# Two small GpSimd steps of an attention's rescaling moved to VectorE, and another order of work at the boundary between heads

## The reference

```python
sim = jnp.einsum('bnkh,bmhk->bnhm', q, k)
attn = jax.nn.softmax(sim * scale, axis=1)
o = jnp.einsum('bnhm,bmhv->bnhv', attn, v)
x = x + ga * (o projected back to width 256)
h = _layernorm(x) * (1 + cb) + sb
x = x + gb * ffn(h)     # gate, up and down with inputs and weights rounded to blockwise FP4
```

## Time and profile before

| | us |
|---|---|
| median of the runs | 1718.21 |
| the profiled execution | 1718.21 |
| its span, first to last instruction | 1716.9 |
| PE busy | 1655.6 (96%) |
| DVE busy | 1591.8 (93%) |
| ACT busy | 1363.7 (79%) |
| POOL busy | 621.7 (36%) |

### The profile page before, as it was taken

The page is one execution under the profiler, slowest core; times in us unless marked ns, Lnnn a source line. Parts: engine busy times, 40 slices in busy tenths (PEclk is TensorE's granted clock), DMA queues, the critical chain, the costliest instruction groups (busy, mean ns, idle before and its releaser), DMA issues.

```text
span 1716.9 us, 37798 instructions
## 1 busy us (share of the span) xinstructions
PE 1655.6 (96%) x15114; PEld 813.1 (47%) x15114; DVE 1591.8 (93%) x1726; ACT 1363.7 (79%) x2488; POOL 621.7 (36%) x1339
## 2 busy tenths in 40 slices
PE   8999999999999999989999999999999989999997
PEld 6643333333333333763333332333333489999997
DVE  7889999999999999779999999999999678888886
ACT  5389999999999999559999999999999633333332
POOL 3023333333333333003633333333333365544442
PEclk9999999999999999999999999999999999999999
DMA  6102111111111112401111111111110422222200
GB/s 228 64 3 64 39 47 32 32 32 40 39 41 40 33 32 62 132 33 47 42 32 32 37 40 38 44 32 32 35 39 21 136 77 74 74 74 77 75 13 19
DMA packets 53018, 89.54 MB, mean 52 GB/s; under 512 B 3298, under 2 KB 34922, under 8 KB 52842
## 3 DMA queue, kind: packets, MB, share of 16 engines
q1 hardware_dynamic: 52426, 86.59, 15.5%
q10 hardware_dynamic: 416, 0.53, 0.1%
HBM read 57.74 MB, written 29.37 MB: 51 GB/s over the span
## 4 chain that ended last, share of the span: by engine, by line
DVE 64%; PE 30%; ACT 3%; issue 2%; POOL 1%; DMA 0%; DVEq 0%; ACTq 0%; POOLq 0%
DVE nm L1043 60%; PE slot L421 9%; PE acc L421 6%; PE acc L582 5%; PE acc L604 5%; ACT e_sb L782 2%; PE slot L638 1%; DVE ost L1056 1%; PE slot L553 1%; DVE v_sb L1004 1%; PE slot L604 1%; PE slot L437 0%; PE acc L615 0%; DVE qs L1110 0%; DVE ost L948 0%
## 5 line engine op out<-in xcount | busy, mean ns | idle before, releaser
L1043 DVE TENSOR_REDUCE nm<-slot 128x1 f32<-128x1024 f32 x1024 | 1166.4, 1215 | 7.5 <-PE slot L553 5.4
L782 ACT ACTIVATE e_sb<-slot,nm 128x1024 f32<-128x1024 f32 x1024 | 1137.4, 1113 | 22.7 <-DVE nm L1043 17.8
L582 PE MATMUL acc<-e_sb,vp 64*64 64x512 f32 x8192 | 1060.6, 594 | 7.0 <-DVE ost L1056 4.7
L553 PE MATMUL slot<-stq,stk 64*64 64x512 f16 x4096 | 411.7, 388 | 21.6 <-ACT e_sb L782 21.6
L553 PEld LDWEIGHTS slot<-stq,stk 64*64 64x64 f16 x4096 | 117.6, 103 | 626.9 <-ACT e_sb L782 589.1
L582 PEld LDWEIGHTS acc<-e_sb,vp 64*64 64x64 f32 x8192 | 283.3, 132 | 188.7 <-issue 74.8
L1259 POOL TENSOR_TENSOR dlt<-nm 128x4 f32<-128x4 f32 x128 | 25.4, 198 | 593.0 <-DVE nm L1043 593.0
L782 ACT ACTIVATION_READ_ACCUMULATOR e_sb<-slot,nm 128x1 f32 x1024 | 199.8, 195 | 0.0
L1250 POOL TENSOR_TENSOR vp<-v_sb,fac 128x512 f32<-128x512 f32 x128 | 133.4, 1042 | 10.1 <-POOL fac L1240 0.2
L1236 POOL TENSOR_TENSOR rtot<-tot,mone 128x4 f32<-128x4 f32 x128 | 131.9, 1030 | 10.0
L1230 POOL TENSOR_TENSOR wsum<-cor,ssum 128x8 f32<-128x8 f32 x128 | 25.9, 202 | 233.5 <-ACT cor L810 233.5
(11 more groups left out here) (168 smaller groups left out, 1759.6 us busy)
## 6 DMA issues: line engine op xcount, KB each, us to landing
stk<-qk_parts SPq DMA_DIRECT2D x128, 128.0 KB
o_heads<-ost SPq DMA_DIRECT2D x64, 256.0 KB, 3.4
v_sb<-o_heads SPq DMA_DIRECT2D x8, 2048.0 KB, 8.2
v_sb<-in_x SPq DMA_DIRECT2D x16, 512.0 KB, 7.7
qk_parts<-e_sb SPq DMA_DIRECT2D x32, 256.0 KB, 2.2
stq<-qk_parts SPq DMA_DIRECT2D x128, 64.0 KB
out<-e_sb SPq DMA_DIRECT2D x32, 128.0 KB, 1.7
v_sb<-in_wgu SPq DMA_DIRECT2D x1, 1408.0 KB, 14.4
```

The source lines that it names most:

```text
L553: mm = pe.matmul(slot[s][side * VD:(side + 1) * VD, c * 512:(c + 1) * 512], stk[c * 64:c * 64 + 64, h % 2, i * P + side * VD:i * P + (side ...
L582: mm = pe.matmul(acc[half * VD:(half + 1) * VD, c * 512:(c + 1) * 512], vp[rows, g % 3, gi, half, :], e_v[rows, j % ERING, n0:n0 + 512], s ...
L782: act.activation(e_v[:, j % ERING, half * 1024:(half + 1) * 1024], slot[u % 3][:, :], ACT.Exp, bias=nm[:, g % 4, i, half:half + 1], accum_ ...
L1043: dve.tensor_reduce(nm[:, g % 4, i, half:half + 1], slot[u % 3][:, :], AX.X, ALU.max, negate=True).then_inc(maxed.sem)
```

## The change

Four edits, all in the attention loop.

1. The cut-off at zero moves from POOL to DVE: at j mod 4 = 0, behind the first maximum. ACT now waits for diff_cut, which DVE signals.
2. The reciprocal of the total moves from POOL (a power of -1) to DVE (a reciprocal): at j mod 4 = 1, behind the first maximum. POOL splits its chain there: wsum and tot at j mod 4 = 0, then fac and vp at j mod 4 = 1 after a wait for rtot_made. The constant mone goes.
3. DVE's copy of acc at the end of a head moves from behind the second maximum to between the two.
4. PE no longer has the special case at the start of a head: each attend call follows its score step there too.

```diff
@@ PE
-                    begins = jv > 0 and jv % NT == 0
                     for half in range(2):
                         if j < JT:
                             scores(b, j, half)
-                        if jv >= 0 and not begins:
-                            attend(b, 2 * jv + half)
-                    if begins:
-                        attend(b, 2 * jv)
-                        attend(b, 2 * jv + 1)
+                        if j >= LAG:
+                            attend(b, 2 * (j - LAG) + half)
@@ ACT
-                        act.wait_ge(*diff_made.past(b * JG + g))
+                        act.wait_ge(*diff_cut.past(b * JG + g))
                         act.activation(cor[:, g % 4], dlt[:, g % 4], ACT.Exp).then_inc(cor_made.sem)
@@ DVE
                 for half in range(2):
+                    if half == 1 and jv >= 0 and jv % NT == NT - 1:
+                        h = jv // NT
+                        dve.wait_ge(*attended.past(b * JT + jv))
+                        if b * H + h >= 2:
+                            dve.wait_ge(*o_out[h % 2].past((b * H + h - 2) // 2))
+                        dve.tensor_copy(ost[:, h % 2, 0:512], acc[:, 0:512]).then_inc(took_low.sem)
                     if j < JT:
                         maximum(b, j, half)
-                if jv >= 0 and jv % NT == NT - 1:
...
+                    if half == 0 and j % GROUP == 0 and GROUP <= j <= JT:
+                        g = j // GROUP - 1
+                        dve.wait_ge(*diff_made.past(b * JG + g))
+                        dve.tensor_scalar(dlt[:, g % 4], dlt[:, g % 4], 0.0, None, ALU.min).then_inc(diff_cut.sem)
+                    if half == 0 and j % GROUP == 1 and GROUP <= j < JT + GROUP:
+                        g = j // GROUP - 1
+                        dve.wait_ge(*tot_made.past(b * JG + g))
+                        dve.reciprocal(rtot[:, g % 4, :], tot[:, g % 4, :]).then_inc(rtot_made.sem)
@@ POOL
-                    sem, n = pool_own.next()
-                    pool.tensor_tensor(tot[:, s, :], wsum[:, s, :, 0], wsum[:, s, :, 1], ALU.add).then_inc(sem)
-                    pool.wait_ge(sem, n)
-                    sem, n = pool_own.next()
-                    pool.tensor_tensor(rtot[:, s, :], tot[:, s, :], mone[:, :], ALU.pow).then_inc(sem)
-                    pool.wait_ge(sem, n)
+                    pool.tensor_tensor(tot[:, s, :], wsum[:, s, :, 0], wsum[:, s, :, 1], ALU.add).then_inc(tot_made.sem)
+                if j % GROUP == 1 and GROUP <= j < JT + GROUP:
                     h, i0 = divmod(GROUP * g, NT)
+                    pool.wait_ge(*rtot_made.past(b * JG + g))
...
-                    pool.tensor_tensor(dlt[:, s, :, 1], nm[:, s, :, 0], nm[:, s, :, 1], ALU.subtract).then_inc(sem)
-                    pool.wait_ge(sem, n)
-                    pool.tensor_scalar(dlt[:, s], dlt[:, s], 0.0, None, ALU.min).then_inc(diff_made.sem)
+                    pool.tensor_tensor(dlt[:, s, :, 1], nm[:, s, :, 0], nm[:, s, :, 1], ALU.subtract).then_inc(diff_made.sem)
```

More of the change, by code:

```diff
@@ L139, in adaln_block @@
         rtot = sb("rtot", [P, 4, GROUP])
-        mone = sb("mone", [P, GROUP])
         fac = sb("fac", [P, 4, GROUP, 2])
@@ L249, in adaln_block @@
         made_ident, made_half, rstd_made, wv_low = tally("made_ident"), tally("made_half"), tally("rstd_made"), tally("wv_low")
-        diff_made, vp_made = tally("diff_made"), tally("vp_made")
+        diff_made, tot_made, vp_made = tally("diff_made"), tally("tot_made"), tally("vp_made")
         wsq_made, root_made = tally("wsq_made"), tally("root_made")
@@ L265, in adaln_block @@
         rows_read, rows_made, gu_quant, dn_quant = tally("rows_read"), tally("rows_made"), tally("gu_quant"), tally("dn_quant")
-        maxed, took_low = tally("maxed"), tally("took_low")
+        maxed, diff_cut, rtot_made, took_low = tally("maxed"), tally("diff_cut"), tally("rtot_made"), tally("took_low")
         wgu_low, wdb_low, x2_made, moments = tally("wgu_low"), tally("wdb_low"), tally("x2_made"), tally("moments")
@@ L670, in tensor_program @@
                         project(1)
-                    jv = j - LAG
-                    begins = jv > 0 and jv % NT == 0
                     for half in range(2):
@@ L1317, in gpsimd_program @@
             pool.memset(quarter4[:, :, :], -0.25)
-            pool.memset(mone[:, :], -1.0)
             pool.memset(epsilon, EPS)
```

## The result

The changed kernel takes 1745.53 us (median of four runs, 1742.92 to 1745.73) against 1718.16 (four runs of the kernel before); the ratio on record is 1.0152, 95% interval 1.0135 to 1.0170, and that of the two medians 1.0159. It is 27.4 us slower. The profiled execution took 1745.73 us, its span is 1744.4, 27.5 more than before. The forecast was 1748 us.

What follows compares the result with a forecast made beforehand. DVE, running its maxima back to back every 1.131 us, was taken as the bound. Terms 21.7 + 0.5 + 7.2 + 0.5 = 29.9 us on top of 1718.21 gave 1748 us, range 1738 to 1757.

Steps and rivals of the forecast that it cites:

- Small instructions: Cut-off and reciprocal on DVE in the attention loop: 124 groups at 0.175 us each, 21.7 us more (17 to 43).
- Rival A: Small instructions on DVE don't overlap with the maxima: 124 x 0.35 = 43.4 us, kernel 1770 us; chance 0.09.
- Waits of the small instructions: In DVE's loop: neither cut-off nor reciprocal waits; the reciprocal has 0.35 us of margin behind POOL's total.
- Rival B: In the loop the reciprocal waits for POOL's total: 19 to 37 us more, kernel 1767 to 1785 us; chance 0.07.
- Folds: Second batch: POOL's folds may hold the reciprocal four times, about 0.3 us each; 0.5 us put down (0 to 1.5).
- Boundary: Between heads: the copy waits 0.44 us, the old 0.20 stall goes; +0.24 us, 30 times, 7.2 us (0 to 13).
- End of the batch: First batch's end: statistics start 2.1 us later, normalisation about 0.5 us later; +0.5 us (0 to 2).
- Rival C: The boundary between heads is cheap: 1741 us, inside the forecast's own range; chance 0.80 together with the forecast.
- D: Rival: not slower; small instructions slip into DVE's waiting time and the 0.2 us stall goes: 1712 us; chance 0.04.

Runs made afterwards that it cites:

- cut_only: The kernel before with only the cut-off at zero moved to DVE, reciprocal on POOL and boundary as before: 1726.63 us, ratio 1.0048.
- recip_only: The kernel before with only the reciprocal moved to DVE, cut-off on POOL and boundary as before: 1727.72 us, ratio 1.0054.
- late2: The changed kernel with two more totals on POOL ahead of the real one, which comes 0.56 us later: 1774.17 us, ratio 1.0321.
- copy_only: The kernel before with only DVE's copy of acc moved between the two maxima: 1728.22 us, ratio 1.0050.
- bound_only: The kernel before with both the moved copy and PE's new attend order, no small instruction moved: 1728.81 us, ratio 1.0050.
- order_only: The kernel before with only PE's new order, each attend behind its score step at a head's start too: 1725.75 us, ratio 1.0036.

## Why the prediction was right

The direction and the mechanism held, and so did the time (1748 against 1745.5), which is partly luck: 3.1 us that the sum did not have stood in for terms that it had too high. Without them the time would be about 1742.4, still in the range. By its terms:

- *Small instructions, 21.7 us.* Measured 16.9. The mechanism was right, the size was off: 0.175 a group was read from starts given to 0.01 us and from other pairs (0.08, where the earlier trace rows have 22.41 - 22.34 = 0.07, and 0.10); between maxima it is 0.070 and 0.085, and of that 0.018 comes back at the maxima behind them. Rival A, the whole length of 0.16 to 0.17 us each, is refuted by the steps of cut_only and recip_only. The prediction read the Trainium skill ("VectorE: DVE Perf Modes", "The DRAIN you can't avoid") without its last sentence: the same paragraph says that a next operation which isn't held starts earlier, so rival A was not what that section makes of this case. The other estimate cited, 17 us by the fixed cycles of "The TRN2 errata", was nearer than the sum's own term: 0.07 + 0.065 us by that section of the Trainium skill, 0.070 and 0.085 less 0.018 measured.
- *Waits of the small instructions: none in the loop.* Right, and so is the margin's size: a total 0.28 us later is free, one 0.56 us later costs 0.23 a group. Rival B came true in late2; by the margin of 0.36 us it would begin with a POOL chain about 0.4 us longer (an estimate).
- *Folds, 0.5 us.* Measured 0. In the profile after, POOL and DVE:

```profile
842.91 0.73 POOL L1204 TENSOR_TENSOR wob<-wo_s,ga 128x256 f32<-128x256 f32 x1
843.32 0.17 DVE L1057 RECIPROCAL rtot<-tot 128x4 f32<-128x4 f32 x1
```

  The reciprocal ran in 0.17 us in the middle of a fold on POOL, as it does four times in this trace (0.165 to 0.168 us each). So it isn't held as the TENSOR_SCALAR of 0.75 us beside POOL's vp was the earlier trace rows, and the second batch's maxima take as long as the first's (614.04 and 614.05). The cut-off ran at the same time as a POOL operation four times and for 0.05 to 0.06 us alone, so whether it would be held is not shown.
- *Boundary, 7.2 us.* Measured 7.0 (30 x 0.234), by the steps as given: the copy waits, 0.40 instead of 0.44; the stall of 0.20 goes, to 0.03. That the wait is 0.40 and not the 0.48 of copy_only and bound_only has a reason in the rows above: a reciprocal (328.00) stands one block before, so DVE comes to the copy 0.06 us later after the maximum on which the attend depends. That is read from the two traces, not tried by itself. The sum had neither the longer wait (0.09 instead of 0.04 us from the attend's end to the copy) nor what shortens it, so part of the agreement is luck.
- *End of the batch, 0.5 us.* Measured 0.45, with the start of the statistics 2.11 us later (3.24 against 1.13) and the second variance no longer held, both as worked out.
- *Not in the prediction:* two stretches at the lower clock, together about 3.1 us. They belong to no edit: the trace of cut_only has none, that of copy_only one, that of order_only two, and executions of the kernel before come with and without them. What makes them come is open; no run varied the idle time ahead of them alone.

The sum is 16.9 + 7.0 + 0.45 + 3.1 = 27.4 us; the forecast's 29.9 was 5.3 too high in the small instructions and the folds, 0.25 too high in the other two terms, and 3.1 too low in the one that was missing. Without the clock's part it stands against 24.3.

Rival C had the boundary nearly free; bound_only, with 37.29 instead of 37.00, is against it. D is refuted by the head of 37.25 us with one small instruction alone.

## What to carry to other kernels

Before moving a small step to another engine, look at the step from start to start of the engine that receives it. If it runs at its own pace (1.8 us idle in 500 instructions here), each instruction costs its start-to-start step, here about half of its length, however much busy time the giving engine loses. And work out the margin of every wait that such an engine gets: here a total 0.28 us later cost nothing, and one 0.56 us later cost 28 us, with a margin of 0.36.

Edits at one place don't add up when each moves the same wait. Copy +0.29, order +0.23, both +0.29.

## What the hardware showed that I had not expected

- The maximum behind a reciprocal is followed after 1.110 us, not 1.131, with a length of 1.193 instead of 1.215; behind the cut-off it is 1.134. So the reciprocal's price is 0.064 us, below that of the cut-off (0.073), though the reciprocal is the longer instruction (0.168 against 0.161).
- A 128x4 reciprocal on DVE is not held by a POOL tensor_tensor of 0.73 us that runs at the same time (four times, 0.17 us long as without).
- Four 64x64 matmuls in different quarters of the array start within 20 to 50 ns, and the next four 0.43 us later. Two of them are followed after 0.21 us by two of the other half, if these stand ready, and otherwise also after 0.43.
- The granted clock fell to 1.2 GHz for 3.4 us about idle times of PE of 0.9 to 2.6 us in the traces of some of these kernels and not of others with the same idle times. Between the batches a drop cost 1.2 to 1.5 us (where it reached into the second batch, part of it stands there), behind the last maximum 1.7 in the mean.
